# Feed-forward network: the first layer of state and twisted state computed once per chunk, and a new order of the chunk pairs

## What is computed

```python
def _twist(x):
    o_r, o_i, p_r, p_i = jnp.split(x, 4, axis=-1)
    return jnp.concatenate([p_r, -p_i, -o_r, o_i], axis=-1)
global_context = x.mean(axis=1, keepdims=True)
gf = _global_net(global_context, gc_w1, ..., gc_b3)
out = x
for _ in range(NUM_CYCLES):            # 3
    tf = _coupling_net(out, cn_w1, ..., cn_b4)
    combined = 0.7 * gf + 0.3 * tf
    coupling = BASE_COUPLING + adaptive_range * (combined - 0.5) * 2.0
    out = out + coupling * _twist(out)
return out
# x = x + _L0_ffn_ref(_layernorm(x), ...)
```

## Time and profile before

| | us |
|---|---|
| median of 3 runs | 2167.82 (2166.8 to 2168.55) |
| the profiled execution, its own time | 2169.16 |
| its span, first to last instruction | 2167.4 |
| busy: PE / DVE / ACT / POOL | 2096.4 / 1773.9 / 1476.9 / 134.3 |
| first feed-forward | first layer from 1474.4, attention b's first turn at 1690.1 |
| second feed-forward | first layer from 1975.0 to the end, 2167.4 |

### The profile page before, as it was taken

How to read it: one execution, slowest core, us unless ns; L and a number is a source line. 1 busy time by engine, 2 the same in 40 slices (tenths; PEclk the granted TensorE clock), 3 DMA queues, 4 the chain that set the end, 5 groups by cost and what they waited for, 6 DMA issues and landing times.

```text
span 2167.4 us, 48580 instructions
## 1 busy us (share of the span) xinstructions
PE 2096.4 (97%) x14502; PEld 882.0 (41%) x14502; DVE 1773.9 (82%) x3326; ACT 1476.9 (68%) x2899; POOL 134.3 (6%) x210
## 2 busy tenths in 40 slices
PE   7799999999999999999999999989999999998998
PEld 4323333333333333333333333244436566664436
DVE  6789999999999999999999999744445677775434
ACT  4438888888888888888888888834555544446653
POOL 1340000000000000000000000010002101002000
PEclk9769999999999999999999999999999999999999
DMA  6421121121121121221221221230000000000002
GB/s 163 142 62 43 46 75 48 47 73 46 49 74 45 50 73 43 53 73 41 54 71 41 56 69 42 58 120 26 1 0 1 1 0 1 0 0 1 0 0 79
DMA packets 93689, 101.24 MB, mean 47 GB/s; under 512 B 35712, under 2 KB 74896, under 8 KB 93552
## 3 DMA queue, kind: packets, MB, share of 16 engines
q1 hardware_dynamic: 93552, 99.79, 16.9%
HBM read 78.72 MB, written 20.71 MB: 46 GB/s over the span
## 4 chain that ended last, share of the span: by engine, by line
PE 88%; ACT 3%; SPq 3%; issue 2%; DVE 2%; DMA 1%; ACTq 0%; POOL 0%; DVEq 0%; POOLq 0%
PE ps L617 22%; PE ps L592 14%; PE ps L640 10%; PE ps L646 10%; PE ps L752 8%; PE ps L760 4%; PE ps L831 2%; PE ps L840 2%; PE ps L860 2%; PE ps L879 2%; ACT YT L1019 2%; PE ps L606 1%; PE ps L910 1%; PE ps L773 1%; PE ps L821 1%
## 5 line engine op out<-in xcount | busy, mean ns | idle before, releaser
L1305 DVE TENSOR_REDUCE mx<-ps 128x1 f32<-128x512 f32 x2048 | 1279.6, 683 | 22.7 <-PE ps L592 18.1
L1019 ACT ACTIVATE YT<-ps 128x512 f32<-128x512 f32 x2048 | 1058.3, 605 | 253.4 <-PE ps L646 253.3
L617 PE MATMUL ps<-YT,work 128*32 128x512 f32 x4096 | 546.2, 605 | 0.0
L592 PE MATMUL ps<-work 64*128 64x512 bf16 x2048 | 462.8, 390 | 11.8 <-DVE mx L1305 8.8
L640 PE MATMUL ps<-work 64*128 64x512 bf16 x2048 | 402.4, 378 | 1.7
L646 PE MATMUL ps<-work 34*128 34x512 bf16 x2048 | 398.9, 378 | 0.0
L592 PEld LDWEIGHTS ps<-work 64*128 64x128 bf16 x2048 | 144.5, 93 | 619.6 <-DVE mx L1305 545.7
L640 PEld LDWEIGHTS ps<-work 64*128 64x128 bf16 x2048 | 162.0, 94 | 106.5 <-ACT YT L1019 31.9
L752 PE MATMUL ps<-YT,c_s 128*128 128x512 f32 x384 | 178.2, 607 | 3.2 <-ACT work L1059 2.5
L617 PEld LDWEIGHTS ps<-YT,work 128*32 128x32 f32 x4096 | 80.7, 108 | 123.0 <-issue 87.3
L646 PEld LDWEIGHTS ps<-work 34*128 34x128 bf16 x2048 | 101.2, 94 | 49.3 <-issue 1.6
(11 more groups left out here) (151 smaller groups left out, 1768.0 us busy)
## 6 DMA issues: line engine op xcount, KB each, us to landing
work<-k_scr SPq DMA_DIRECT2D x640, 64.0 KB, 2.2
work<-q_scr SPq DMA_DIRECT2D x640, 32.0 KB, 1.8
o_scr<-o_sb SPq DMA_DIRECT2D x32, 256.0 KB, 2.2
X<-in_L_attn_a_x_dram SPq DMA_DIRECT2D x8, 512.0 KB, 7.2
work<-negt SPq DMA_DIRECT2D x256, 1.0 KB
work<-o_scr SPq DMA_DIRECT2D x16, 256.0 KB
work<-inv_scr SPq DMA_DIRECT2D x16, 256.0 KB
out_dram<-X SPq DMA_DIRECT2D x16, 256.0 KB, 2.1
```

What stands on the lines that cost most here:

```text
L592: mm(ps[:, bank_of[x], :], qa[rows, p, jp, qt * P:(qt + 1) * P], ka[rows, p, kc_ * CH:(kc_ + 1) * CH], start=True, stop=True).then_inc(a_m ...
L617: m = mm(ps[32 * j:32 * j + 32, 7, :], vst[:, p, t, :], prob(GROUP * t + j), start=t == 0, stop=t == KTILES - 1)
L1019: fn(prob(u), ps[:, S_BANK + u % S_RING, :], ACT.Exp, scale=HD ** -0.5).then_inc(exp_ok, 1)
L1305: dve.tensor_reduce(mx[:, p, at_:at_ + 1], ps[:, bank_of[x], :], AX_X, ALU.max).then_inc(a_max, 1)
```

## The change

It rests on twist(twist(x)) = -x. With A the first layer's product of the normalised state and B that of the twisted state, cycle 0 needs A, cycle 1 needs A + c0 B, and cycle 2 needs A + c0 B + c1 (B - c0 A).

1. PE computes A (cycle 0, weights `c1_s`) and B (cycle 1, weights `ct_s`, the twisted rows of the same matrix with signs, made once on DVE). Cycle 2 has no first layer. The sum is kept in `summed(c)`, in buffers of attention a that are free by then (`vals`, `part_b`).
2. ACT copies A out of PSUM (128x1024, new L1135) after its gelu. For cycles 1 and 2 the gelu reads `summed(c)` in SBUF instead of PSUM and waits for DVE's `update`.
3. DVE's `update` works on 128x1024: in cycle 1 four instructions (product c0 A into `YT`, product c0 B out of PSUM, the sum, and B - c0 A into `YT`), in cycle 2 two.
4. The state is never turned back. The three couplings of a token combine to two factors, alpha-like for its own row and beta-like for the twisted row. Cycles 0 and 1 give their tanh by tokens through DRAM: SP stores row 0 of `th` (4 KB) and loads it as 128x8 single words (`by_token`); POOL makes the factors (`token_parts`, 9 small instructions a pair). Cycle 2's fourth layer is computed with tokens on the partitions (`w4_s`, four matmuls of 2 columns a pair). DVE's `last_coupling` (5 small instructions a pair) joins the three.
5. Then ACT's `turned_rows` makes the scaled row (four of 128x256 a chunk) and DVE's `joined` updates `X` (four tensor_scalar of 128x256 and four tensor_tensor of 128x4x64 a chunk). `rejoin` and `rejoined` are gone. The output is stored a whole chunk at a time.
6. The order of the pairs is a table, `PAIRS`; None is a pair of slots without items. 26 slots instead of 24, and lags of 5 to 9 slots for the steps behind an item.
7. The global network of the first batch starts in slot 3 instead of 5, and POOL's `root` makes the shift also for stage 1.

```diff
-GLOBAL_AT = (5, 9)
+GLOBAL_AT = (3, 8)
+PAIRS = ((0, 0), (0, 1), (0, 2), (1, 0), (1, 1), (0, 3), (2, 0), (2, 1), (1, 2), (1, 3), None, (2, 2), (2, 3))
+T_LAG, U_LAG, J_LAG, N_LAG, R_LAG = 5, 6, 7, 8, 9
...
+                        if b_ == 0:
+                            wait(pe, f_as, k * NCH + begun(n))
+                            wait(pe, f_d, k * NCH + middles(n - 1))
+                        else:
+                            wait(pe, f_d, k * NCH + middles(n - 1))
...
+                        if y == 0:
+                            act.wait_ge(f_h1, k * 2 * NCH + firsts(n + 1))
+                        else:
+                            act.wait_ge(f_up, k * 2 * NCH + updates(n + 1))
...
+                        if y == 0:
+                            act.copy(summed(c), ps[:, 0:KT, :]).then_inc(f_as, 1)
...
-                    if n % 2 == 0 and n - 4 >= NCH:
-                        coupled(n - 4, n - 3)
+                    if n % 2 == 1 and is_update(n + 1):
+                        coupled(n + 1)
+                        coupled(n + 2)
...
+                def update(n):
+
+                    y, c = ORDER[n]
+                    p, done = updates(n) % 2, k * 2 * NCH + updates(n + 1)
+                    by = cs[:, updates(n) % 4, :].rearrange("p (a n) -> p a n", a=1).broadcast_to((P, KT, CH))
+                    own, at_ = YT[:, :, ch(c)], first_bank(n)
+                    dve.wait_ge(f_cs, done)
+                    if y == 1:
+                        dve.wait_ge(f_h1, k * 2 * NCH + firsts(n + 1))
+                        dve.tensor_tensor(own, by, summed(c), ALU.mult)
+                        dve.tensor_tensor(tw[:, p], ps[:, at_:at_ + KT, :], by, ALU.mult).then_inc(f_tw, 1)
+                    else:
+                        dve.tensor_tensor(tw[:, p], own, by, ALU.mult).then_inc(f_tw, 1)
+                    dve.wait_ge(f_tw, done)
+                    dve.tensor_tensor(summed(c), summed(c), tw[:, p], ALU.add).then_inc(f_up, 1)
+                    if y == 1:
+                        dve.tensor_tensor(own, ps[:, at_:at_ + KT, :], own, ALU.subtract).then_inc(f_d, 1)
...
+                def joined(c):
...
+                    for t in range(4):
+                        m = dve.tensor_scalar(X[:, 4 * c + t, :], X[:, 4 * c + t, :], v4[:, c, 0, t:t + 1], v4[:, c, 1, t:t + 1],
+                                              ALU.mult, ALU.add)
...
+                    for q, of, op in ((0, 2, ALU.add), (1, 3, ALU.subtract), (2, 0, ALU.subtract), (3, 1, ALU.add)):
+                        m = dve.tensor_tensor(quarters[:, :, q, :], quarters[:, :, q, :], turned_x[c % 2][:, :, of, :], op)
...
+                sp.dma_start(z_tok[:, y, own, :].rearrange("p c t -> p (c t)"),
+                             tokens.rearrange("(x p) -> p x", p=P), allow_slow_non_contiguous=True).then_inc(zt_ld[q], 16)
```

More of the change, by code:

```diff
@@ L58 @@
 S_BANK, S_RING = 3, 4
-GLOBAL_AT = (5, 9)
-Y_LAG = 6
-LAG = 3
+GLOBAL_AT = (3, 8)
+PAIRS = ((0, 0), (0, 1), (0, 2), (1, 0), (1, 1), (0, 3), (2, 0), (2, 1), (1, 2), (1, 3), None, (2, 2), (2, 3))
+ORDER = tuple((pair[0], 2 * pair[1] + o) if pair else None for pair in PAIRS for o in range(2))
+SLOTS = len(ORDER)
+T_LAG, U_LAG, J_LAG, N_LAG, R_LAG = 5, 6, 7, 8, 9
 TILES = TOKENS // P
@@ L272, in hybrid_block @@
         x_ld = [sem(f"x_ld{c}") for c in range(NCH)]
+        zt_ld = [sem(f"zt_ld{q}") for q in range(NCH // 2)]
         def ch(c):
@@ L338, in through_tiles, with firsts, updates, middles @@
                 visit(n, n % 2, 0)
+        def firsts(n):
+            return sum(1 for item in ORDER[:max(n, 0)] if item and item[0] < CYCLES - 1)
+        def updates(n):
+            return sum(1 for item in ORDER[:max(n, 0)] if item and item[0] > 0)
+        def middles(n):
+            return sum(1 for item in ORDER[:max(n, 0)] if item and item[0] == 1)
+        def items(n):
+            return sum(1 for item in ORDER[:max(n, 0)] if item)
+        def begun(n):
+            return items(n) - updates(n)
+        def ended(n):
+            return items(n) - firsts(n)
+        def first_bank(n):
+            return 5 * (n % 2) if ORDER[n][0] == 1 else 0
+        def is_item(n):
+            return 0 <= n < SLOTS and ORDER[n] is not None
+        def at_end(n):
+            return is_item(n) and ORDER[n][0] == CYCLES - 1
+        def is_update(n):
+            return is_item(n) and ORDER[n][0] > 0
         def wait(eng, s, value):
@@ new lines, in layers @@
+                    if is_item(n - 1):
+                        act.wait_ge(f_h2, base + items(n))
+                        wait(act, f_h3, pairs + items((n - 5) // 2 * 2 + 2) // 2)
+                        fn(h2[:, (n - 1) % 4, :], ps[:, 2, :], ACT.Gelu, bias=bias[:, D2:D2 + 1]).then_inc(f_a2, 1)
+                    if n % 2 == 1 and is_item(n - 3):
+                        act.wait_ge(f_h3, pairs + items(n - 1) // 2)
+                        wait(act, f_z, pairs + items(n - 5) // 2)
+                        fn(h3[:, (n // 2 - 1) % 2, :], ps[:, 3, :], ACT.Gelu, bias=bias[:, D3:D3 + 1]).then_inc(f_a3, 1)
@@ new lines, in layers @@
+                    if n % 2 == 0 and is_item(n - 4):
+                        act.wait_ge(f_z, pairs + items(n - 2) // 2)
+                        y, c = ORDER[n - 4]
+                        if y == CYCLES - 1:
+                            fn(z_end[:, c:c + 2, :], ps[:, 4, 0:8].rearrange("p (t o) -> p o t", o=2), ACT.Tanh,
+                               bias=half_b[:, 0:1], scale=0.5).then_inc(f_ze, 1)
+                        else:
+                            if y == 1:
+                                act.wait_ge(z_st, 16 * (k * NCH + firsts(ORDER.index((0, c))) // 2 + 1))
+                            for o in range(2):
+                                fn(th[:, c + o, :], ps[:, 4 - o, :], ACT.Tanh, bias=half_b[:, 0:1], scale=0.5).then_inc(f_th, 1)
@@ L1650, in _ @@
                 root(3, c)
+            for q in range(NCH // 2):
+                token_parts(1, q)
 _INS = ['L0_attn_a_x', 'L0_attn_a_Wq', 'L0_attn_a_bq', 'L0_attn_a_Wk', 'L0_attn_a_bk', 'L0_attn_a_Wv',
```

383 lines of the change are left out of this document (210 added, 173 removed).

## The result

| | us |
|---|---|
| median before, in the comparison of both kernels | 2167.82 |
| median after, 5 runs | 2159.22 (2156.87 to 2159.75) |
| ratio after to before, 95% interval | 0.9955 (0.9944 to 0.9967) |
| the profiled execution of after, its own time and its span | 2156.87 and 2154.9 |

What follows compares the result with a forecast made beforehand. PE bounds the kernel now; after the change DVE and ACT set the schedule. Savings of 17.0 (second feed-forward) and 12.7 (first), together 29.7, less 5.4 for clock drops, give 24.3 off 2167.8: 2143.5 us, range 2122 to 2163.

Steps and rivals of the forecast that it cites:

- Slots 16 to 19: Cycle 1, second batch: first layer, update and gelu stand in a row, 13.7 us a pair, 27.3 in all.
- DVE's joins: Tail, chunks 4 to 7: bound by DVE, 2.8 us a join, plus 1.75 of moments each in the first feed-forward.
- the store: End of the second feed-forward: the last chunk's 512 KB stored at once, 3.5 us, between 2.6 and 5.2.
- the rival of the slow load: Loading 1024 single words by tokens takes twelve us more per feed-forward and eats the gain; chance 0.09 with similar stalls.
- The sign against: Over the middle of the feed-forwards, a PEclk (granted PE clock) under 0.9 would show the forecast wrong.
- The first step that failed: the clock: PE waits in thin stretches of both feed-forwards; three clock drops of up to 1.8 us on the path, 5.4 in all.
- My reason against: Against clock drops in every thin stretch: a window with PE busy half of its time stayed at clock 1.00.
- the clock falls in every thin stretch: Rival: drops in six thin stretches of both feed-forwards cost 21.6 us instead of 5.4, giving 2159.7; chance 0.18.
- Slots 0 to 5: Start of each feed-forward: +3.1 us, 1.0 for slot 1 waiting for the copy, 2.1 for couplings before slot 6.
- Slots 6 to 16: From slot 6's first layer to slot 16's, over cycles 1, 0 and 2 of the first batch: 55.9 us.
- Last tanh: After the last first-layer gelu: second, third and fourth layers with activations, 5.7 and 5.9 us to the last tanh.
- Behind the last spread: End of the first feed-forward: silus now stand behind that spread, so attention b begins 4.4 us after it, before 2.7.

Runs made afterwards that it cites:

- the runs above: Follow-up runs of the changed kernel, one repeated without an edit (2157.22 us), the others with fillers or reordered steps (2126.64 to 2157.24 us).
- the filled run: Changed kernel in its own order, with unread matmuls on PE in every gap where any of its profiles showed the clock fall: 2145.75 us, ratio 0.9904.
- the two profiled executions: The changed kernel profiled, then once more without an edit: medians 2159.22 and 2157.22 us, spans 2154.9 and 2155.2 us.

## Why the prediction missed

Of the 24.3 us forecast, 15.7 did not come. Two things failed: the price of the clock, about 6 of them, and terms of the schedule itself, about 10.

**Right.** The common frame was: PE's saved work does not show as such, DVE and ACT set the new schedule. Slots 16 to 19 (13.7 a pair) and the way from there to the last gelu came out within 0.7 us. So did DVE's joins (20.3 forecast from the last tanh to the last moments in the first feed-forward, 1678.26 - 1657.41 = 20.9 measured) and the store (3.5, measured 2154.9 - 2151.5 = 3.4). The load by tokens landed in a median of 2.3 us; POOL alone waited for it, and DVE's `last_coupling` waited for ACT's tanh and not for POOL, so the rival of the slow load falls.

```profile
z_tok<-z_scr SPq DMA_DIRECT2D x16, 4.0 KB, 2.3
```

Of the signs named beforehand, first layers in slots 6 to 9 came 6.4 to 6.8 apart (6.4 forecast), the pairs of cycle 2 10.7 us apart in the first feed-forward and 9.0 in the second (9 forecast), and attention b 0.3 us later instead of 12 to 13 earlier. The sign against, a PEclk under 0.9 over the middle, stayed silent: from slot 6 to the last gelu PEclk was 0.92 and 0.94, and 0.87 and 0.91 only with the ends. It was set too low to warn.

**The first step that failed: the clock, 5.4 taken, 11 to 12 measured by filling.** I had counted three drops at 1.8. In after the rows show on the path 3.08 in slot 1 (before already lost 1.70 of this there, so 1.4 more), 1.28, 1.69 and 1.58 in the last cycle of the first batch, 0.92 and 0.78 in the last fourth layers, for instance

```profile
1655.23 1.87 PE L862 MATMUL ps<-w_s,work 128*128 128x2 f32 x8 [0.78 <-ACT work L1143]
```

and behind the last spread this:

```profile
1684.10 3.75 PE L900 MATMUL ps<-lqk_s,work 128*128 128x512 f32 x4 [5.23 <-ACT work L1205]
1687.64 1.90 PE L617 MATMUL ps<-ident,xn 128*128 128x128 f32 x8
```

1.87 and 0.8. Together about 10.3 that before does not lose, and with its 1.7 in slot 1 about 12, near what filling gave back. Half-clock second layers in slots 23 and 24 (3.78, 3.27, and 3.78, 3.49) cost nothing: with them at full clock that stretch is 34.0 and 26.4 us as well. My reason against, the window that stayed at 1.00 with PE half busy, was a piece of a gap of 1.64 us, seen in one execution. The rows around it in the kernel before, all at full clock:

```profile
1678.22 1.09 PE L537 MATMUL ps<-ident,xn 128*128 128x128 f32 x8 [1.09 <-ACT xn L1038]
...
1682.67 1.09 PE L537 MATMUL ps<-ident,xn 128*128 128x128 f32 x8 [1.64 <-ACT xn L1038]
1685.62 1.96 PE L831 MATMUL ps<-lqk_s,work 128*128 128x512 f32 x4 [1.86 <-ACT work L1120]
```

That such gaps passed there says little: in the same execution the wait of 1.93 us did not pass, and in the runs above waits of 2.2 to 2.9 us stood ahead of slow and of fast instructions. The rival "the clock falls in every thin stretch" stood at 2159.7, and 2159.22 was measured, but only half of that agreement is earned: its price of 21.6 was about twice too high, and the other terms made up for it. The Trainium skill (TensorE: Matmul & The Clock Gate, HAM oscillation) says, of a kernel that waits for DMAs, that bursts between long waits each begin slow; the traces here, with waits for ACT, agree in kind, not burst by burst (1.95 behind a wait of 2.88 in one place, 3.23 in the other).

**The second: other terms of the sum, about 10 us, the larger part of what is missing.** That they were too small is read from the stretches of the filled run; apart from slots 0 to 5, no run tests one of them alone.
- Slots 0 to 5: the copy's 1.0 and the couplings' 2.1 came as worked out (the waits rose by 0.91 and by 2.17). Left out was that all three layers of the global network now stand ahead of slot 6, where two did (slots 2 to 5 are 0.8 us longer), and that the longer wait in slot 1 is paid at half clock.
- Slots 6 to 16: 57.3 at full clock against 55.9. That is 1.4 us in both feed-forwards; the second network's small matmuls on PE, which I left out, make some 1.0 of it, handoffs the rest.
- Last tanh: I took 5.7 and 5.9 us. The last pair's third layer also waits for the pair before it, whose tanh by tokens ends only 4 us before the last; 7.3 at full clock (first feed-forward; the 9.3 of the second holds the drop that was left and a filler).
- Behind the last spread: I only moved the silus there. The second one needs a projection of its own, and that stands on PE behind the wait for the first. 8.3 us forecast from the last moments to attention b, 12.2 measured in after, of which 2.7 are the half clock counted above, and 9.7 with the gaps filled.
- A term in my favour was mis-sized as well. A pair of gelus out of SBUF took 1.33 and not 1.51:

```profile
2060.87 1.33 ACT L1131 ACTIVATE work<-vals,bias 128x512 f32<-128x512 f32 x2 [1.91 <-DVE vals L1485]
```

The row of 1.51 was an instruction with a scale for each partition besides the bias, so it differed from the gelu in more than its source. A pair out of SBUF cost 0.06 more than out of PSUM. Here the figure of the Trainium skill (VectorE: DVE Perf Modes, The TRN2 errata), by which I had estimated a third of the row's 0.24, was nearer. Its double speed for tensor_scalar (The perf-mode tier table) did not show: four took 1.35 to 1.38, as the row said, and four tensor_tensor of the same size 1.43. What the cheaper gelus gave back, some 3 us by the forecast's own estimate, is in the filled column, so the missing terms are larger than they look by that much.

**What the forecast could have seen** is in its own table of slots. It noted that the joins of chunks 2 and 3 stand ahead of updates 22 and 23, and priced it; it did not ask whether anybody needs them there. Nor did it ask whether slot 1 must wait for the copy, which it also priced, or could use free banks. The two moves that ask this (joins later with the couplings earlier; slot 1 in free banks with the put first) are worth 17 us, twice the change.

## What to carry to other kernels

Work taken off the busiest engine turns into gaps, and here a gap could be paid twice, as waiting and as half clock behind it: price the second part from every gap of the new schedule, not from the few that one execution shows slow. Where PE must wait a few microseconds anyway, matmuls that nobody reads were worth 4 to 11 us in 2157; where they were longer than the gap they cost what stuck out, about 1 us in one slot. And in an engine's queue, work that nobody waits for belongs behind what the chain needs: moving two joins in each feed-forward back by two or three slots, with the couplings brought forward, gave 6 us.

## What the runs showed of the hardware

- Where the clock falls differs between executions of one program (slot 1's first layer 6.75 and 3.67 us, slot 6's 3.67 and 5.37), while the spans of the two profiled executions agree within 0.3 us. A single profile therefore does not price a single gap.
- A small instruction of GpSimd ran up to twice as long beside VectorE's. Two roots in the changed kernel, the first beside the second half of an update (128x1024) and a join, the second beside nothing but a memset:

```profile
1630.92 2.13 POOL L1670 TENSOR_TENSOR norm<-var,mhalf 128x4 f32<-128x4 f32 x1
...
1678.65 1.01 POOL L1670 TENSOR_TENSOR norm<-var,mhalf 128x4 f32<-128x4 f32 x1
```

Beside joins and moments alone a root took 1.17 to 1.18. The slow one cost nothing here, since ACT was busy with other work until after its end.
